# The causal mask of an attention score tile: two float32r matmuls inside the tile against two bfloat16 matmuls at the end of its slot

## The reference

```
x = x + attention(layernorm(x));  x = x + ffn(layernorm(x))
q, k, v = split(x @ qkv_w + qkv_b)                    # 16 heads, D = 64
logits  = q @ k.T / sqrt(64)
logits  = where(tril(ones(2048, 2048)), logits, large_negative)
attn    = softmax(logits) @ v;   out = attn @ out_w + out_b
```

## Time and profile before

| what | value |
|---|---|
| median of 3 runs | 998.61 us (998.5 to 1002.36) |
| the profiled execution | 999.62 us, of which the span of its instructions is 997.8 us |
| PE busy over the span | 94% |
| DVE, ACT, POOL busy | 74%, 71%, 73% |
| attention (first scores to last PV products) | about 63 to 822 us of the span |
| one head | about 46.3 or 48.4 us, by turns |

### The profile page before, as it was taken

The page is one execution under the profiler, slowest core; times in us unless marked ns, Lnnn a source line. Parts: engine busy times, 40 slices in busy tenths (PEclk is TensorE's granted clock), DMA queues, the critical chain, the costliest instruction groups (busy, mean ns, idle before and its releaser), DMA issues. The chain is left out here.

```text
span 997.8 us, 25979 instructions
## 1 busy us (share of the span) xinstructions
PE 935.9 (94%) x10330; PEld 793.1 (79%) x10330; DVE 741.6 (74%) x1775; ACT 713.4 (71%) x891; POOL 729.9 (73%) x460
## 2 busy tenths in 40 slices
PE   7889999999999999999999999999999976679992
PEld 6558888888888888888888888888888765569992
DVE  4978696868778786878697869686876478656664
ACT  3038888888788788788878788888888853426661
POOL 1328878888888889888988897888789956154442
PEclk7769999999999999999999999999999979879996
DMA  3321434343534344444522241404030306011214
GB/s 104 84 53 34 94 77 115 80 108 77 117 78 108 79 116 94 110 89 112 108 75 66 75 93 41 111 29 102 1 87 5 133 6 249 25 49 57 58 55 134
DMA packets 70103, 82.03 MB, mean 82 GB/s; under 512 B 8784, under 2 KB 53970, under 8 KB 67936
## 3 DMA queue, kind: packets, MB, share of 16 engines
q1 hardware_dynamic: 67712, 76.14, 31.0%
q0 software_dynamic: 2272, 4.24, 1.2%
HBM read 21.81 MB, written 25.30 MB: 47 GB/s over the span
## 5 line engine op out<-in xcount | busy, mean ns | idle before, releaser
L583 POOL TENSOR_TENSOR p_lo<-prob,p_hi 128x1024 f16<-128x1024 f32 x320 | 617.2, 1947 | 144.8 <-ACT p_hi L685 143.5
L684 ACT ACTIVATE prob<-st,p_bias 128x1024 f32<-128x1024 f32 x320 | 330.0, 1031 | 131.2 <-PE st L1276 106.8
L685 ACT ACTIVATE p_hi<-st,p_bias 128x1024 f16<-128x1024 f32 x320 | 328.1, 1025 | 0.0
L979 DVE TENSOR_REDUCE row_max<-bg 128x1 f32<-128x512 f32 x384 | 255.7, 686 | 15.8 <-PE bg L1201 10.8
L1275 PE MATMUL st<-big 128*128 128x512 f32 (+3 forms) x640 | 246.8, 386 | 2.5 <-ACT p_hi L685 1.6
L1300 PEld LDWEIGHTS pv<-v_parts,p_hi 128*128 128x128 f16 x2176 | 198.1, 96 | 56.8 <-issue 33.3
L1201 PE MATMUL bg<-big 128*128 128x512 f32 (+3 forms) x640 | 240.2, 407 | 2.7 <-DVE v_parts L969 2.1
L1300 PE MATMUL pv<-v_parts,p_hi 128*128 128x65 f16 x2176 | 236.6, 195 | 1.8 <-POOL p_lo L583 1.8
L1276 PE MATMUL st<-big 65*128 65x512 f32 (+3 forms) x640 | 236.3, 369 | 0.0
L1302 PE MATMUL pv<-v_parts,p_hi 128*128 128x64 f16 x2176 | 234.1, 195 | 0.0
L1304 PE MATMUL pv<-v_parts,p_lo 128*128 128x65 f16 x2176 | 232.4, 192 | 0.0
(11 more groups left out here) (224 smaller groups left out, 1214.4 us busy)
## 6 DMA issues: line engine op xcount, KB each, us to landing
big<-big SPq DMA_DIRECT2D x192, 128.0 KB, 2.3
row_dram<-fill SPq DMA_DIRECT2D x8, 1300.0 KB, 9.2
big<-part_dram SPq DMA_DIRECT2D x8, 1088.0 KB, 7.9
big<-big SPq DMA_DIRECT2D x16, 512.0 KB, 4.3
part_dram<-stage_parts SPq DMA_DIRECT2D x32, 176.0 KB, 2.6
part_dram<-stage_parts SPq DMA_DIRECT2D x16, 192.0 KB, 3.7
stage_raw<-ffn_w SPq DMA_DIRECT2D x16, 176.0 KB, 3.0
v_parts<-row_dram SPq DMA_DIRECT2D x39, 65.0 KB
```

Source lines behind the costliest of these rows:

```text
L583: nc.gpsimd.tensor_tensor(o, a, b, ALU.subtract).then_inc(p_lo_ready, 1)
L684: nc.scalar.activation(o32, src, ACT.Exp, bias=p_bias[:], scale=D ** -0.5)
L685: nc.scalar.activation(o16, src, ACT.Exp, bias=p_bias[:], scale=D ** -0.5).then_inc(exp_done, 1)
L979: nc.vector.tensor_reduce(row_max[:, t, c:c + 1], bank, AX_X, ALU.max).then_inc(bg_drained, 1)
```

## The change

The two mask operands become bfloat16 (0, 1 and -1e30 rounded to bfloat16; they were float32r), and the two mask matmuls of a diagonal slot move out of `scores` into `masks(n)`, which is called after the tail and before the PV products. `st_ready` of such a slot is raised by the second of them. Slots without a diagonal raise it as before.

```
-        ident_r = sb("ident_r", [P, P], F32R)
-        mask_cols_r = sb("mask_cols_r", [P, P], F32R)
+        ident_b = sb("ident_b", [P, P], BF16)
+        mask_cols_b = sb("mask_cols_b", [P, P], BF16)
...
-            nc.scalar.copy(ident_r[:], ident[:]).then_inc(consts, 1)
+            nc.scalar.copy(ident_b[:], ident[:]).then_inc(consts, 1)
             act.wait_ge(masks_ready, 2)
-            nc.scalar.copy(mask_cols_r[:], mask_cols[:]).then_inc(consts, 1)
+            nc.scalar.copy(mask_cols_b[:], mask_cols[:]).then_inc(consts, 1)
...
-                if diagonal:
-                    j = kt - 4 * b
-                    mm = nc.tensor.matmul(st[:, n % STRING, k, tile(j)], ident_r[:], mask_cols_r[:],
+                if k == 1 and not diagonal:
+                    mm.then_inc(st_ready, 1)
+
+            def masks(n):
+
+                b, p = GROUPS[n]
+                if p < 2 * b:
+                    return
+                for k in range(2):
+                    j = 2 * p + k - 4 * b
+                    mm = nc.tensor.matmul(st[:, n % STRING, k, tile(j)], ident_b[:], mask_cols_b[:],
                                           start=False, stop=True)
-                if k == 1:
-                    mm.then_inc(st_ready, 1)
+                mm.then_inc(st_ready, 1)
...
                     for task in SLOTS[h][n][second_at:]:
                         background_task(task)
+                    masks(n)
```

## The result

The changed kernel takes 992.51 us in the median of 8 runs (989.48 to 997.25), the kernel before 999.11 beside it (8 runs, 997.99 to 1002.36): a ratio of 0.9930, 95% interval 0.9913 to 0.9947, so 5 to 9 us less. A second series gave 991.83 us and 0.9924 (0.9895 to 0.9953). The forecast was 986.1, 12.5 us less, with a range up to 994. The profiled execution took 994.17 us.

What follows compares the result with a forecast made beforehand. The prediction took PE to bound the attention. Removing 27.4 us of masks, adding 14.1 us of new ones and losing 0.8 us to a bank wait gave -12.5 us: 986.1 us, range 983.5 to 994.

Steps and rivals of the forecast that it cites:

- rival 1: New masks' weight loads not quite hidden, steps about 0.08: a saving of 6.1 us, 992.5 us; chance 0.11.
- Rival 2: All diagonal slots with a tail give their 0.115 back as bank waits: 5.6 us more, 991.7 us; chance 0.07.
- What bounds: In the attention PE is busy 749.3 of 759 us, so a step it does not take is time saved.
- What is removed: 256 float32r masks in 128 diagonal slots: 96 pairs at 0.225 and 32 at 0.18, 27.4 us.
- what is added: 256 bfloat16 masks of 128 columns before PV, loads hidden: 0.11 us a pair, 14.1 us.
- My own sign for a wrong count: Masks at 0.06 but under 8 us saved would mean the count for removed float32r masks is wrong.
- The 81 ns a pair of the Trainium skill: Rule for sustained load and matmul at 128 columns: masks would cost 20.7 us instead of 14.1; given a small chance.
- I count no loss: In odd heads' slot 4 the matching DVE task starts behind a mask and moves with it: no bank-wait loss.
- The loss in slot 4 of even heads: PE waits for DVE to empty a bank, so the slot's saving is lost: 7 x 0.11 = 0.8 us.
- The late `st_ready`: In slots with a tail it comes later, 0.56 in the worst; ACT's idle time and the ring hide it: no cost.
- Rival 4: Scores two slots behind a tail wait because `st_ready` comes late: 18 us more, 1004 us; chance 0.04.
- POOL's margin in slot 19: POOL's lead before the PV products shrinks from 0.43 to 0.25 us, with no time lost.

Runs made afterwards that it cites:

- experiment 5: The changed kernel with each mask added twice, four masks a slot; 1004.40 us, ratio 1.0025 against the kernel before.
- experiment 4: The changed kernel with its two mask matmuls left out; 983.51 us, ratio 0.9833 against the kernel before.
- experiment 1: The kernel before with only the mask type changed to bfloat16, masks in their old place; 1001.61 us, ratio 0.9997.
- experiment 10: The kernel before again, unchanged, for a second profile, on a slower chip; 1010.28 us in one run.
- experiment 6: The changed kernel with its masks in front of the tail instead of behind it; 994.36 us, ratio 0.9932 against the kernel before.
- experiment 9: The changed kernel with scores first in even heads' slot 5 and masks before the tail in odd heads' slot 11; 998.11 us, slower chip, ratio 0.9902.

## Why the prediction was right in kind and twice too large

The number came out within the range only because that was drawn up to 994 for rivals 1 and 2. The forecast's own part, 983.5 to 989.5, was missed by 3 us, and neither rival came true as written: that the total lies inside is in part luck. By steps:

- **What bounds: right for heads 0 to 14, wrong in four slots of the last.** Two more masks take 0.09 to 0.12 in seven of the eight diagonal slots of even heads (experiment 5), and two fewer give 0.10 to 0.12 in six (experiment 4). In the last head slots 4 and 5 run at ACT's pace, 2.01 us whatever the masks cost. The four waits for exponentials of the earlier trace rows were read and not taken out of the sum.
- **What is removed, 27.4 us, and what is added, 14.1 us: right, slightly high.** The middle task's and the tail's steps went back as forecast; a pair of new masks is 0.12 less 0.01 of the first PV step. In slots with no wait the net gain is 0.10 to 0.12 where I had 0.115, and 0.05 to 0.08 where I had 0.07. Heads 0 to 14 miss about 1 us by this in the first profile and 0.7 in the second. My own sign for a wrong count, masks at 0.06 and a total that fell by less than 8 us, came up (6.6 us), and it pointed the wrong way: experiment 4 confirms the count, and the time went where PE waits.
- **The 81 ns a pair of the Trainium skill: not borne out.** Two masks take 0.12, 0.067 and 0.056; four take 0.23. What looked like rival 1 in the total (992.5 forecast for it, 992.5 measured) was not rival 1: its sign, steps of 0.08, is absent.
- **"I count no loss" in odd heads: this step failed.** Rival 2 named the mechanism and not the place. I had checked bank waits only where the trace before showed one already; slot 11 of odd heads showed none and had a margin of 0.14. The load came to want the bank 0.09 earlier, DVE emptied it 0.11 later in the slot, and the slot lost all its 0.11: 7 x 0.11 = 0.8 us. The loss in slot 4 of even heads was forecast, and it was exactly that (0.00 saved).
- **DMA landings: not looked for.** The prediction followed banks, ACT and POOL, but not `k_lo_landed`. Slot 4 of the seven odd heads together stayed 1.1 us below the forecast in the first profile and 0.8 in the second, for late copies in heads 5 and 11 above all. Copies are as late in experiments 1 and 10, where the masks stand in the old place, so it is not shown that the change makes them late; that the first profile before had no such wait is chance, and it makes the gain look smaller.
- **The last head: mis-sized.** I gave it 0.8 us of gain like the others. It lost 1.6 and 0.5 us, so 2.4 and 1.3 us of what is missing: 0.5 in slots 1, 4, 5 and 19, which PE does not bound, 0.6 by the wait in slot 13, where one more small DVE operation was caught behind POOL (0.85 us), 0.2 in slot 10, and in the first profile 1.1 by the time at which the clock rises again, which is chance.
- **The late `st_ready`, cost nothing: right.** PE's waits for L685 are 1.7 us, 1.6 before, and raising it earlier (experiment 6) brings nothing. Rival 4 is out.
- **POOL's margin in slot 19: right.** Slot 19 gains 0.10 in even and odd heads, and in head 8 0.26 of margin is left where I had 0.25. Without the new masks it is used up in even heads (experiment 4).

The sum for the first profile: 12.5 forecast - 1.0 - 0.8 - 1.1 - 2.4 = 7.2, as measured. For the second: 12.5 - 0.7 - 0.8 - 0.8 - 1.3 = 8.9, where 8.8 was measured. Both are accounts after the fact, slot by slot; only the wait in slot 11 was also taken away by experiments (5, 6 and 9). How much of the landings and of the last head recurs from run to run stays open; the medians of two series, 6.6 and 9.2 us lower than before, lie about those sums.

## What to carry to other kernels

A short matmul is paid by the weight loads around it: put short 2-byte matmuls next to other 2-byte ones, and count both its own step and what its neighbour pays. When work leaves a saturated engine, list for every wait behind it in the same stretch how late its releaser is (banks, DMA landings, an engine's chain), not only the waits that already show; the margin is eaten by what was removed in front of the wait, in its own slot and in the slots before that its releaser does not gain, even if something is added again behind it. A change worth a few tenths of a microsecond in each of many repeats is best read from slot lengths in two profiles, since a whole run varies by more.

## What the runs showed of the hardware

- A wait for a bank holds up the weight load, not only the matmul: a float32r load that started 0.11 late had its 512-column matmul step 0.34 instead of 0.24 (slot 11, head 7 of the changed kernel).
- A bfloat16 mask between float32r matmuls steps 0.04, less than its 128 columns do elsewhere (0.056), and the matmul behind it takes 0.08 more (experiment 1), though the prediction had said that no mask can be shorter than its columns; together that is what a float32r mask costs.
- DVE operations on 8 elements a partition took 1.02 to 2.04 us instead of 0.17 when they ran into a POOL subtraction (last head of the changed kernel).
